# Low half of the transposed context: from VectorE out of PSUM to GpSimd out of SBUF rows

## The reference

```python
x = x + _L0_xattn_ref(_layernorm(x, axis=-1), ctx_2048)
x = x + _L0_ffn_ref(_layernorm(x, axis=-1), gate_w, w_gate, w_up, w_down, sw_gate, sw_up, sw_down)

def _L0_xattn_ref(x, weight):
    xq = quant_dequant_act_1x128(x)            # float8 e4m3, one scale per row and 128 columns
    wq = quant_dequant_weight_128x128(weight)  # float8 e4m3, one scale per 128x128 block
    return jnp.einsum('emk,enk->emn', xq, wq)
```

## Time and profile before

| what | value |
|---|---|
| three runs | 6593.26, 6591.76, 6581.7 us |
| median | 6591.76 us |
| the profiled execution | 6590.12 us, span 6588.2 us |
| granted TensorE clock, mean | 0.992 of full speed |
| TensorE busy | 96% of the span; two tenths in the first of 40 slices, nine or more in the next 38 |
| VectorE, ScalarE, GpSimd busy | 30%, 20%, 44% |

### The profile page before, as it was taken

How to read it: one execution, slowest core, us unless ns; L and a number is a source line. 1 busy time by engine, 2 the same in 40 slices (tenths; PEclk the granted TensorE clock), 3 DMA queues, 4 the chain that set the end, 5 groups by cost and what they waited for, 6 DMA issues and landing times.

```text
span 6588.2 us, 89812 instructions
## 1 busy us (share of the span) xinstructions
PE 6347.2 (96%) x32166; PEld 3137.9 (48%) x32167; DVE 2004.7 (30%) x2640; ACT 1330.1 (20%) x1976; POOL 2900.1 (44%) x2388
## 2 busy tenths in 40 slices
PE   2999999999999999999999999999999999999998
PEld 1555544445554444444444444444444444444443
DVE  7888533211112222232222222232222332223220
ACT  2666622110001111111111111111111111111111
POOL 4444523732002444454445444454444545445453
PEclk9999999999999999999999999999999999999999
DMA  2455544544335555666666565676655666667653
GB/s 87 154 156 155 178 129 88 122 108 132 109 98 152 158 159 159 164 177 176 168 171 166 164 159 158 166 196 178 170 161 158 184 192 170 168 164 187 180 151 94
DMA packets 1122342, 1015.67 MB, mean 154 GB/s; under 512 B 875504, under 2 KB 877808, under 8 KB 1122288
## 3 DMA queue, kind: packets, MB, share of 16 engines
q1 hardware_dynamic: 177920, 437.40, 20.3%
q10 hardware_dynamic: 838720, 241.77, 19.5%
q0 software_dynamic: 105648, 335.82, 16.5%
HBM read 623.21 MB, written 210.14 MB: 126 GB/s over the span
## 4 chain that ended last, share of the span: by engine, by line
PE 73%; POOL 6%; issue 5%; DVE 5%; DMA 4%; ACTq 3%; ACT 3%; POOLq 0%; DVEq 0%; SPq 0%
PE ps_gu L766 48%; PE ps_d L766 23%; DMA out<-s_out,y_now 3%; PE ps_d L969 2%; ACTq L1228 2%; POOL s_out L701 1%; POOL list_rows L652 1%; POOL hid L711 1%; ACTq L1246 1%; POOL hid_hl L716 1%; ACT wts L1117 1%; DVE wts L1452 1%; DMA xT<-xin 1%; POOL s_out L694 1%; ACT dout L1262 1%
## 5 line engine op out<-in xcount | busy, mean ns | idle before, releaser
L766 PE MATMUL ps_gu<-wts,xT 128*128 128x512 f16 (+1 forms) x20304 | 3950.6, 356 | 24.4 <-DMA xT<-xin 8.2
L766 PEld LDWEIGHTS ps_gu<-wts,xT 128*128 128x128 f16 x20304 | 1993.4, 98 | 1947.1 <-issue 27.4
L766 PE MATMUL ps_d<-wts,hT 128*128 128x512 f16 x7968 | 1768.1, 380 | 23.4 <-ACT dout L1262 11.9
L1594 DVE TENSOR_SCALAR wts<-stage 128x1408 f16<-128x1408 f32 (+2 forms) x447 | 427.6, 957 | 3180.8 <-PE ps_d L969 2995.4
L766 PEld LDWEIGHTS ps_d<-wts,hT 128*128 128x128 f16 x7968 | 778.8, 98 | 956.8 <-issue 38.7
L701 POOL TENSOR_TENSOR s_out<-s_out,dout 128x1024 f32<-128x1024 f32 x208 | 529.7, 2547 | 1218.9 <-ACT dout L1262 1215.8
L1596 DVE SCALAR_TENSOR_TENSOR wts<-stage,wts 128x1408 f16<-128x1408 f32 (+2 forms) x447 | 735.7, 1646 | 15.4
L1232 ACT ACTIVATE sil<-ps_gu 128x704 f32<-128x704 f32 (+2 forms) x272 | 199.1, 732 | 2023.8 <-PE ps_gu L766 2023.6
L1262 ACT ACTIVATE dout<-ps_d,lists 128x1024 f32<-128x1024 f32 x208 | 231.8, 1114 | 1349.7 <-issue 1338.3
L1238 ACT ACTIVATE hid_hl<-hid 128x704 f16<-128x704 f32 (+2 forms) x272 | 207.9, 764 | 1284.8 <-POOL hid L711 1224.0
L711 POOL TENSOR_TENSOR hid<-hid,sil 128x704 f32<-128x704 f32 x208 | 348.5, 1675 | 131.7 <-ACT hid L1266 127.4
(11 more groups left out here) (167 smaller groups left out, 2650.4 us busy)
## 6 DMA issues: line engine op xcount, KB each, us to landing
stage<-in_L_ffn_w_down SPq DMA_DIRECT2D x384, 256.0 KB, 4.4
stage<-in_L_ffn_w_gate SPq DMA_DIRECT2D x256, 352.0 KB, 4.0
stage<-in_L_ffn_w_up SPq DMA_DIRECT2D x256, 352.0 KB, 5.6
wts<-in_x SPq DMA_DIRECT2D x64, 512.0 KB, 3.7
rows_x<-wts SPq DMA_DIRECT2D x64, 512.0 KB, 3.2
xT<-cols_x ACTq DMA_DIRECT2D x63, 512.0 KB
wts<-in_ctx SPq DMA_DIRECT2D x32, 512.0 KB, 4.0
cols_x<-xT SPq DMA_DIRECT2D x32, 512.0 KB, 4.7
```

The lines of the kernel that those rows point to most:

```text
L766: ins = nc.tensor.matmul(dst[c], left, right[c], start=(first and a == 0), stop=(last and a == 2))
L1594: v.tensor_scalar(high, raw, WSCALE, 1.0, ALU.mult, ALU.mult).then_inc(cast_done, 1)
```

## The change

GpSimd makes the low half, from SBUF rows in place of the PSUM tile and the scales. For that ScalarE writes the scaled chunk into SBUF as full float32 rows (`ctx_f`, 128x1024, in the tile `hT`, whose part used by the slice lies behind it), waits for that, and copies it as float16 into `cT`. GpSimd then subtracts the one from the other (`ctx_low`), once for the whole chunk and not by blocks. The PSUM tile is free (`ctx_taken`) once ScalarE has read it. `ctx_f` is free again, and the chunk done, with `ctr_free`, which GpSimd now raises. VectorE's eight instructions per chunk go, and its four loops over the tiles become two. On GpSimd the new step stands behind `unround_ctx` and ahead of `split_slice` (first 8 chunks) or of `low_of_x2` (tiles 0 to 23). The last of the first 8 chunks stands behind `dequantise_x(0)` and ahead of the last two splits.

```diff
+        ctx_f = hT_flat[:, 0:2 * H].bitcast(F32).rearrange("p (k n) -> p k n", k=KH)
...
@@ gpsimd
+            def ctx_low(c, j, b):
+                pool.wait_ge(ctx_high, c + 1)
+                pool.sem_inc(pool_turn, 1)
+                g.tensor_tensor(cT[b % 2][:, 1, :, ds(j * P, P)], ctx_f, cT[b % 2][:, 0, :, ds(j * P, P)],
+                                ALU.subtract).then_inc(ctr_free, 1)
...
-            def beside(i, ctx=True, x2=True):
+            def beside(i, ctx=True, x2=True, low=None):
                 dequantise_x(i + (LEAD - 1))
                 if ctx:
                     unround_ctx(i + (CLEAD - 1))
+                if low is not None:
+                    ctx_low(i + BT, *low)
                 if x2:
                     low_of_x2(i)
             for c in range(BT):
                 unround_ctx(c)
+                if c > 0:
+                    ctx_low(c - 1, c - 1, 0)
                 split_slice(c)
             dequantise_x(0)
+            ctx_low(BT - 1, BT - 1, 0)
             for c in range(BT, CHUNKS_S):
                 split_slice(c)
...
@@ tensor
             def tr_ctx(c):
                 pe.wait_ge(deq_ready[CTX], c + 2)
-                pe.wait_ge(ctr_free, c + 1)
+                pe.wait_ge(ctx_taken, c + 1)
@@ scalar
             def take_ctx(c, j, b):
                 act.wait_ge(ctr_done, c + 2)
+                act.wait_ge(ctr_free, c + 1)
                 act.sem_inc(act_turn, 1)
                 for k in range(KH):
-                    last = a.activation(cT[b % 2][:, 0, k, ds(j * P, P)], ps_t_ctx[:, k, :], ACT.Copy, scale=scale_of_ctx(c, k))
-                last.then_inc(ctx_high, 1)
+                    last = a.activation(ctx_f[:, k, :], ps_t_ctx[:, k, :], ACT.Copy, scale=scale_of_ctx(c, k))
+                last.then_inc(ctx_taken, 1)
+                act.wait_ge(ctx_taken, c + 2)
+                act.sem_inc(act_turn, 1)
+                a.activation(cT[b % 2][:, 0, :, ds(j * P, P)], ctx_f, ACT.Copy).then_inc(ctx_high, 1)
@@ vector
-            def ctx_low(c, j, b):
-                dve.wait_ge(ctx_high, c + 1)
-                dve.sem_inc(dve_turn, 1)
-                for k in range(KH):
-                    last = v.scalar_tensor_tensor(out=cT[b % 2][:, 1, k, ds(j * P, P)], in0=ps_t_ctx[:, k, :],
-                                                  scalar=scale_of_ctx(c, k), in1=cT[b % 2][:, 0, k, ds(j * P, P)],
-                                                  op0=ALU.mult, op1=ALU.subtract)
-                last.then_inc(ctr_free, 1)
...
-                if low is not None:
-                    ctx_low(i + BT, *low)
```

More of the change, by code:

```diff
@@ L269, in build @@
             for n in ("qin_in", "qin_free", "rounded", "deq_ready"))
-        unrounded_x, ctx_high = sem("unrounded_x"), sem("ctx_high")
+        unrounded_x, ctx_taken, ctx_high = sem("unrounded_x"), sem("ctx_taken"), sem("ctx_high")
         q_high = sem("q_high")
@@ L621, in _ @@
             beside(-1, x2=False)
[L622 to L625, removed]
+            beside(0, low=(0, 1))
+            beside(1, low=(1, 1))
+            with pool.Fori(2, BT) as i:
+                beside(i, low=(i, 1))
+                add_slice(i - 2)
+            with pool.Fori(BT, 2 * BT) as i:
+                beside(i, low=(i - BT, 2))
+                add_slice(i - 2)
+            with pool.Fori(2 * BT, TT - CLEAD + 1) as i:
+                beside(i, low=(i - 2 * BT, 3))
                 add_slice(i - 2)
@@ L629, in _ @@
                 if i < TT - LEAD + 1:
-                    beside(i, ctx=False)
+                    beside(i, ctx=False, low=(i - 2 * BT, 3) if i < 3 * BT else None)
                 else:
@@ L1074, in _ @@
             act.sem_inc(tr_free, 1)
+            act.sem_inc(ctx_taken, 1)
             act.sem_inc(norm_l, 1)
@@ L1508, in between, with beside @@
                 yield
-            def beside(i, x=True, ctx=True, low=None, sliced=True):
+            def beside(i, x=True, ctx=True, sliced=True):
                 if ctx:
@@ L1539, in _ @@
                 quantise(c=c)
-                ctx_low(c - 1, c - 1, 0)
             x_moments(0)
@@ L1543, in _ @@
             quantise(0)
-            ctx_low(BT - 1, BT - 1, 0)
             for i in (1, 2):
@@ L1552, in _ @@
                     low_of_q(0)
[L1553 to L1560, removed]
+            beside(0, sliced=False)
+            beside(1, sliced=False)
+            with dve.Fori(2, TT - CLEAD) as i:
+                beside(i)
             with dve.Fori(TT - CLEAD, 3 * BT) as i:
-                beside(i, ctx=False, low=(i - 2 * BT, 3))
+                beside(i, ctx=False)
             with dve.Fori(TT - BT, TT - LEAD) as i:
```

## The result

| | median | runs | profiled execution |
|---|---|---|---|
| before | 6590.02 us (6581.7 to 6598.8) | 7 | 6590.12, span 6588.2 |
| after | 6608.60 us (6601.5 to 6615.7) | 7 | 6610.45, span 6608.8 |

The ratio is 1.0032, with a 95% interval of 1.0021 to 1.0043. So the change costs 0.3%, or 18.6 us between the medians. The forecast was 6611.

A forecast was written before the change was run, and what follows sets the result against it. The prediction took a chain of waits as the bound: VectorE in the context chunks, VectorE and ScalarE in series in the tiles. 6.0 - 0.7 + 13.8 = +19.1 us gave 6611, range 6586 to 6624.

The forecast's parts named there:

- Stage A: Batch 0's eight context chunks up to the first attention product: GpSimd's subtraction and VectorE hold each other up, +6.0 us.
- The last splits falling into tile 1's quantisation: Before the first attention product: one delayed GpSimd split falls among VectorE's locking instructions, +4.2 us.
- L1438 locks, by likeness to L1452: Context chunks: this VectorE instruction, two SBUF operands, cannot run beside GpSimd's; pass 11.1 us, or 10.0 if it can.
- Rival 2: L1438 runs free of GpSimd and ScalarE's wait on itself costs nothing: +12 us, 6604; chance 0.13.
- Tiles 0 and 1: First two attention tiles, without silu: VectorE's low half was on the chain, so its removal gains 0.35 us each, -0.7.
- Stage B: Attention tiles 2 to 21: ScalarE's wait and copy, 1.15 us less 0.41 covered, lengthen each tile; +13.8 us in all.
- GpSimd's 2.12 in stage B costs nothing, boundaries nothing: Attention tiles: GpSimd's 2.12 us subtraction fits its idle time; nothing counted at batches' first tiles, up to 3 us each otherwise.
- A microsecond gained or lost earlier is passed on whole: After about 700 us, where TensorE or GpSimd's weight splits bind: earlier gains or losses reach the end undiminished.
- Rival 1: VectorE's relief wins in the context chunks, up to -15 us there, total 6590; decides from passes of about 9.2; chance 0.17.
- Rival 4: Attention tiles: the copy costs nothing because TensorE ends each tile; total +5 us, 6597; chance 0.05.
- rival 5: Whole kernel: VectorE's relief wins at the start and the copy costs nothing; -16 us, 6576; chance 0.05.
- Rival 3: Copy charged in full (25 us in tiles) and GpSimd's low half late at batch boundaries (9): +39 us, 6631; chance 0.10.

The follow-up runs named there:

- e6: Changed kernel without GpSimd's subtraction in the first eight chunks (ScalarE writes a second copy, result wrong); first attention product at 109.65 us, against 119.09 changed, 117.33 before.
- e8: Changed kernel with 16 TensorE products that nobody reads after each attention product of tiles 3 to 21; 6605.0 us, ratio 1.0026 to before.
- e7: Changed kernel with ScalarE's copy made twice in each of tiles 0 to 23; 6639.1 us, ratio 1.0073 to before.
- e3: Changed kernel with ScalarE's copy behind x2's high half and GpSimd's subtraction behind L610, except in each batch's last tile; 6596.1 us, ratio 1.0011.
- e9 to e12: x's maxima and scaling moved earlier: changed kernel with late copy 6545.6, also with old start and some early copies 6541.6, kernel before 6545.8, changed kernel 6557.9 us.

## Why the prediction was right, and where its terms were off

The time (6611 for 6608.6) and the mechanisms came as forecast. Two terms were mis-sized in opposite directions, by 4 and 8 us, and that they offset each other in part is luck. At tile 22 the forecast is still 4 us short (19.1 for 23.2); that it fits the medians owes to the rest of the run, on which see below, and to the 7 runs' median of before, 1.7 us under that of the first three.

- **Stage A, +6.0 forecast, +1.76 measured.** The mechanism held in its order (L1442 held by the low half, L1447 by the split's first piece, L1452 by the second, the third ahead of L1457); e6 proves the cause. The size of the passes was off: +2.4 forecast up to the eighth chunk's maxima, measured 75.81 to 74.45, -1.36. I let each of VectorE's instructions wait for a whole piece, but a piece has begun while VectorE is at something else, so that only 0.30 and 0.40 of a 0.65 piece are waited for: +0.17 a pass and not +0.74. And only four passes are so long, not five: up to the third chunk's maxima the change gave 1.6 (23.99 to 22.41) and not 1.3, and the third pass, which I had among the long ones, another 0.5. Tile 0's quantisation: -0.6 forecast, -0.25 measured (tile 1's maxima, 104.22 to 102.61, against the -1.36). The last splits falling into tile 1's quantisation: +4.2 forecast, +3.4 measured.
- **"L1438 locks, by likeness to L1452": right**, and so does L1443, a single operand in SBUF: 0.69 became 1.59. Rival 2's half lock is out.
- **Tiles 0 and 1, -0.7 forecast**: 41.42 us after against 42.16 before. Right.
- **Stage B, +13.8 forecast, +22.0 measured.** The step that the copy lies whole in front of the roots, less 0.41 that covers it, is right: 1.06 + 0.21 - 0.41 = 0.86, measured 0.87 and 0.86 (e8). The wait of ScalarE on itself, bounded by nothing and 0.2 and taken as 0.1, is 0.21, the upper bound: +2.2 over 20 tiles. TensorE absorbed nothing of it, where I had taken 1 off: +1. The rest is a term that I did not have: what lies above 20 ordinary tiles, 6.2 us after (501.4 less 20 x 24.76) and 1.6 before (479.4 less 20 x 23.89), so +4.6. The seven long tiles with slow transposes make 5.9 of the 6.2, the two before 1.2 of the 1.6. Together 13.8 + 2.2 + 1 + 4.6 = 21.6.
- **GpSimd's 2.12 in stage B costs nothing, boundaries nothing**: right. L605 is 2.13, and GpSimd's idle time before L610 fell from 13.6 to 12.0. The first products of the second and fourth batch wait 0.23 and 2.88 for L605, where they waited 0.76 and 2.82 for L1396. TensorE waiting for L605 there, which I had named a sign of being wrong, does occur, but costs nothing more than before.
- **"A microsecond gained or lost earlier is passed on whole": not decided.** The lag is 23.2 us at tile 22, 24.5 at tile 31 and 20.6 at the end. Behind tile 31's residual the profiled execution of the kernel before took 5726.0 us and that of the kernel after 5722.1. But in the experiments, whose program is the same there, it took 5711.7 to 5731.9 (e6 aside, which chooses other experts), so 4 us lie inside what single executions differ by.
- **The rivals.** Rival 1 had the right doubt about stage A: pieces that hold VectorE less than counted; but its point of decision was a pass of 9.2, and the pass was 10.53. Rival 4 is out by e7 and e3, and rival 5 with it. Rival 3's 25 us for an uncovered copy came near in size (22), by another way.

What stays open: why one tile has slow transposes and the next not. The ordinary tile above had 2.79 us of idle time before L806 and the slow one only 1.92, so the idle time just before does not decide it by itself. Shown is that they come more often when ScalarE's chain is longer (e7), and vanish, but for tile 3 of e8, with more work and less idle time of TensorE in the same stretch, by needless products (e8) or a denser tile (e9 to e12). Which of the two it takes was not tested.

## What to carry to other kernels

Before work is moved between engines, ask which engine's program stands in series with the rest: here 1.27 us on a ScalarE that was two thirds busy cost 0.87 a tile, and the 2.2 us taken off a VectorE nine tenths busy gave nothing. The same work in another place of the same engine's program cost an ordinary tile nothing (e3), though the batch boundaries paid for it. Where an instruction waits for "issue", look at what the queue in front of it waits for: one exchange of two ScalarE steps, with the VectorE step that feeds it moved up too, was worth 2 us a tile, twice what the change under study had cost.

## What the runs showed of the hardware

- ScalarE waiting for its own last result costs 0.20 to 0.21 us (L1115), more than the 0.15 between dependent small instructions of VectorE.
- Several of VectorE's instructions with SBUF operands and GpSimd's take turns, even one of 128x8 (L1442, 0.17 became 1.32) and one of a single input (L1457, 0.69 became 1.59), and GpSimd is held as well (L561, 1.22 became 2.06). Not all do: the reduction L1406 took its 1.21 beside GpSimd's L600. A held instruction waits for the rest of one already under way (0.30 and 0.40 of pieces of 0.65). The Trainium skill, "SBUF — State Buffer", section *Who interferes with whom*, tells of this turn-taking as an exclusive lock on a shared port pair; the rows agree.
- Eight transposes of 128x128 took 1.09 us at a granted clock of 1.00 and 1.83 us in a stretch of 0.57, behind idle time of TensorE. A chain through another engine then begins late, and 0.7 us of a slower clock become 0.9 us of a longer tile. With sixteen needless products in the gap the granted clock of 400 to 600 us was 1.00 in place of 0.97, and twenty tiles took 6.7 us less.
